# Summing the state outputs by accumulating transfers into two sums per chunk, with all steps written out

## The chip, the cores and the metric

One core of a Trainium2 chip runs the kernel. The metric is device time in microseconds (us), from the runs' own measurement; the profile is of one further execution of the same program. Engines are named as in the profile: PE (TensorE, matmuls), DVE (VectorE), ACT (ScalarE), POOL (GpSimd), SP (SyncE, which issues the plain transfers).

## What is computed

Four residual blocks over x of shape (4, 1024, 256), each followed by a layer norm: a gated linear recurrence, a ReLU feed-forward block, a selective state space block, and a second feed-forward block. The change lies in the third. Cut to what matters:

```python
dA  = exp(dt[..., None] * A)                    # (B, T, D, N), N = 16 states
dBx = dt[..., None] * B_ssm[:, :, None, :] * x_conv[..., None]
h_t = dA_t * h_(t-1) + dBx_t                    # a scan over time, for each channel and state
y_t = einsum('bdn,bn->bd', h_t, C_t)            # sum over the 16 states
y   = y * silu(z);  out = y @ out_proj_w.T
```

## The kernel before

The 4 sequences of 1024 tokens are cut into 8 chunks of 512 tokens (T). Channels lie on partitions: 256 channels are H = 2 halves of 128 partitions, so that a chunk's tile is 128 partitions x 1024 floats, 4 KB per partition and 512 KB in all. The program is software-pipelined over steps. In step i five stages of different chunks run side by side: *ahead* (chunk i+1: loads and first convolution), *gate* (chunk i: the recurrence of block one, out projection, first feed-forward up), *prep* (chunk i-1: feed-forward down, inputs of the state space block, the softplus for dt), *scan* (chunk i-2: the 16 states) and *tail* (chunk i-3: readout, out projection, second feed-forward, store). Each engine has its own instruction list; the function `step` of each engine writes out by hand in which order the pieces of these five stages follow one another, and semaphores tie the engines together. An engine works strictly in its order.

Four steps (3 to 6) are run by an engine loop of two turns (`Fori` in `steps`, two steps in a turn), the others are written out.

For one state n of a chunk in the scan stage:

- PE spreads the rows of B and C over 128 partitions into PSUM (L1287), ACT makes dA (L660).
- DVE `state_input` multiplies u by B into PSUM (L968, two instructions), `state_scan` runs the recurrence of both halves (L981), `state_output` multiplies the state by C into slot n % CRING of the ring hC (L994). The ring has CRING = 4 slots.
- POOL `sum_states` (L378) adds the slot to y, for n = 1 to 15: 15 additions of 128x1024 floats per chunk, each after the last. `state_output` of state n waits until the addition of state n-4 has read its slot:

```python
if n >= CRING:
    dve.wait_ge(S["y_sum"], ADDS * c + max(n - CRING, 1))
```

- DVE `readout` (L1000) multiplies the finished y by the gate, in the next step, after state 1 of the next chunk.

POOL also does, in the same hand-written order: the row scales of four layer norms (`row_scales`, L293 to L299, which wait for DVE's moments L843), the additions of two convolutions (`conv_add` L316, `mconv_add` L326), residuals and biases (L339, L342, L306), parts of log1p (`log1p_parts`, L350 to L360: maximum, minimum and two steps of a series) and the copies of the last state column (`save_carry` L386). In this order `sum_states(scan, 8)` stands behind the gate stage's `row_scales`, and `sum_states(scan, 9)` behind `log1p_parts`. DVE does, beside the states, the recurrence of block one (`log_A` L867, `recurrence` L903), moments of the layer norms (L836, L843), and a number of products of two SBUF tiles (L895, L936, L941, L951, L955, L1000).

Of the kernel before, what the change touches and what calls it, by code (L numbers as in the profile page):

```python
# [29 lines left out]
P = 128  # L30
D = 256
H = D // P
# [14 lines left out]
HRING = 2  # L47
CRING = 4
ARING = 4
BRING = 3  # L50
ADDS = NS - 1

# [12 lines left out]
LAGS = LAG_AHEAD, LAG_GATE, LAG_PREP, LAG_SCAN, LAG_TAIL = -1, 0, 1, 2, 3  # L65
LOOP_FIRST, LOOP_PAIRS = 3, 2


def build(nc, xT, x, par, ffb, rows, gateT, outT, inT, xpT, opT, w1a, w2a, w1b, w2b, out):
    ctx = ExitStack()  # L70
    with ctx:
# [57 lines left out]
        dt = sb("dt", [P, H, T])  # L129
        u = [sb(f"u{n}", [P, H, T]) for n in range(2)]  # L130

# [3 lines left out]
        carry = sb("carry", [P, NS, H])  # L135
        y = sb("y", [P, H, T])
        yg = sb("yg", [P, H, T])
# [25 lines left out]
        def input_banks(n):  # L163
# [11 lines left out]
            dt_ready u_ready  # L175
            B_mm C_mm dA_ready dBx_ready h_ready carry_saved hC_ready y_sum yg_ready eps_ready tau_set ln_tau_ready x3_seeded xtok_loaded passed
            op_mm x3T_mm x3T_ready x3b_ready up1_mm relu1 down1_mm stored""".split()
        S = {n: sem(n) for n in names}
        weight_loaded = {n: sem(f"{n}_loaded") for n in "gate xp out w1_0 w2_0 in op w1_1 w2_1".split()}
        xt_loaded = [sem(f"xt_loaded{n}") for n in range(2)]  # L180

        sum_ready, stats, meanvar, neg_ready, ve_ready, rstd_ready, shift_ready, norm_ready = (
# [5 lines left out]
        def steps(eng, step):  # L188


            def chunk(i):
                return (i // PER_SEQ, i % PER_SEQ) if 0 <= i < NCHUNK else None

            def straight(i):
                step(*(chunk(i - lag) for lag in LAGS))

            for i in range(LAG_AHEAD, LOOP_FIRST):
                straight(i)
            with eng.Fori(0, LOOP_PAIRS) as turn:
                for k in range(PER_SEQ):  # L200
                    def at(lag):
                        i = LOOP_FIRST + k - lag
                        return (turn + i // PER_SEQ, i % PER_SEQ)
                    step(*(at(lag) for lag in LAGS))
            for i in range(LOOP_FIRST + PER_SEQ * LOOP_PAIRS, NCHUNK + LAG_TAIL):
                straight(i)

        def apart(eng):


            eng.sem_inc(S["passed"], 1)

        def num(ch):
# [60 lines left out]
        def _(pool):  # L274
# [94 lines left out]
            def sum_states(ch, n):  # L369

                c = num(ch)
                if n == 1 and not first(ch):
                    pool.wait_ge(S["yg_ready"], c)
                pool.wait_ge(S["hC_ready"], UNITS * c + H * n + H)
                if n > 1:
                    pool.wait_ge(S["y_sum"], ADDS * c + n - 1)
                so_far = hC[:, 0, :, :] if n == 1 else y[:]
                nc.gpsimd.tensor_tensor(y[:], so_far, hC[:, n % CRING, :, :], ALU.add).then_inc(S["y_sum"], 1)  # L378

# [7 lines left out]

            def step(ahead, gate, prep, scan, tail):
                if scan is not None:
                    save_carry(scan, 0)  # L390
                    save_carry(scan, 1)
                    sum_states(scan, 1)
# [406 lines left out]
        def _(dve):  # L799
# [153 lines left out]
            def dt_x(ch):  # L953
                dve.wait_ge(S["dt_ready"], num(ch) + 1)
                V.scalar_tensor_tensor(out=u[ch[1]][:], in0=dt[:], scalar=0.5, in1=v[:], op0=ALU.mult,  # L955
                                       op1=ALU.mult).then_inc(S["u_ready"], 1)


            def state_input(ch, n):

                c = num(ch)
                if n == 0:
                    dve.wait_ge(S["u_ready"], c + 1)
                else:
                    dve.wait_ge(S["hC_ready"], UNITS * c + H * n)
                dve.wait_ge(S["B_mm"], NS * c + n + 1)
                for h in range(H):
                    V.tensor_tensor(input_banks(n)[h][:], u[ch[1]][:, h, :], B_bank(n)[:], ALU.mult).then_inc(S["dBx_ready"], 1)  # L968

# [14 lines left out]
            def state_output(ch, n):  # L984
                c = num(ch)
                dve.wait_ge(S["C_mm"], NS * c + n + 1)

                if n >= CRING:
                    dve.wait_ge(S["y_sum"], ADDS * c + max(n - CRING, 1))
                elif not first(ch):  # L990
                    dve.wait_ge(S["y_sum"], ADDS * c + n + 1 - CRING)
                for h in range(H):
                    dve.wait_ge(S["h_ready"], UNITS * c + H * n + h + 1)
                    V.tensor_tensor(hC[:, n % CRING, h, :], hs[:, n % HRING, h, :], C_bank(n)[:], ALU.mult).then_inc(S["hC_ready"], 1)  # L994

            def readout(ch, gate):
                if gate is not None:
                    dve.wait_ge(S["conv_sum"], PAD * (num(gate) + 1))
                dve.wait_ge(S["y_sum"], ADDS * (num(ch) + 1))
                V.scalar_tensor_tensor(out=yg[:], in0=y[:], scalar=0.5, in1=zz[ch[1]][:],  # L1000
                                       op0=ALU.mult, op1=ALU.mult).then_inc(S["yg_ready"], 1)
# [502 lines left out]
```

## Time and profile before

| | |
|---|---|
| time, median of 3 runs | 1121.71 us (1120.54 to 1122.82) |
| span of the profiled execution, first to last instruction | 1118.2 us |
| what lies around the span, against the median | 3.5 us |
| DVE busy | 911.4 us, 82% of the span |
| PE busy (matmul) | 831.4 us, 74% |
| POOL busy | 688.4 us, 62% |
| ACT busy | 634.9 us, 57% |
| bytes moved by DMA | 19.42 MB, 17 GB/s over the span |

The profile of before does not state the profiled execution's own total time apart from its span; the span and the median of the runs are 3.5 us apart. Busy shares are of the whole span. The scans of the eight chunks run from about 170 to 1058 us; before them the pipeline fills, after them the last chunk's tail stage stands alone.

### The profile page before, as it was taken

The numbers are of one execution on the slowest core, as the hardware profiler recorded it, in microseconds if no ns is written. First come the engines' busy times: TensorE is split into PE (matmuls) and PEld (weight loads), VectorE is DVE, ScalarE is ACT, GpSimd is POOL, SyncE is SP. The second block draws the span as 40 slices with busy tenths as digits, with TensorE's granted clock in tenths as the row PEclk, the third lists the DMA queues.
The fourth block names the chain that finished last, engine by engine and source line by source line (L and its number), as shares of the span: only waits on it lengthen the run. The fifth ranks groups of instructions, "written<-read, shape, count | busy, mean of one in ns | idle before, by whom it ended". The sixth has DMA issues, their size and how long they took to land. (4 is left out here: it accounts for less than half of the span.)

```text
span 1118.2 us, 9795 instructions
## 1 busy us (share of the span) xinstructions
PE 831.4 (74%) x2536; PEld 501.1 (45%) x2536; DVE 911.4 (82%) x1250; ACT 634.9 (57%) x1016; POOL 688.4 (62%) x460
## 2 busy tenths in 40 slices
PE   2368469647877997798869986988788888269376
PEld 1126226223634664465436543656354645035144
DVE  0303227999999999999999999999999999999911
ACT  3533564747376756686668657766746376334221
POOL 2131373669755995689567967796749575845410
PEclk9779769767988998899889989999988889559678
DMA  8000000000000010001000000001000000000000
GB/s 300 0 19 19 0 20 19 1 19 0 1 1 0 1 57 1 1 1 58 1 0 0 23 34 0 0 0 38 1 1 1 19 1 1 19 1 0 19 1 19
DMA packets 9219, 19.42 MB, mean 17 GB/s; under 512 B 1360, under 2 KB 3920, under 8 KB 9168
## 3 DMA queue, kind: packets, MB, share of 16 engines
q1 hardware_dynamic: 9168, 18.88, 5.0%
q14 instruction: 36, 0.29, 0.1%
q8 instruction: 15, 0.25, 0.1%
HBM read 14.68 MB, written 4.19 MB: 17 GB/s over the span
## 5 line engine op out<-in xcount | busy, mean ns | idle before, releaser
L378 POOL TENSOR_TENSOR y<-y,hC 128x1024 f32<-128x1024 f32 x112 | 295.3, 2637 | 56.5 <-DVE hC L994 53.5
L1287 PE MATMUL pBC<-stack,sel 97*128 97x512 f32 x256 | 156.5, 626 | 119.5 <-DVE hs L981 116.2
L660 ACT ACTIVATE dA<-dt,A_neg 128x512 f32<-128x512 f32 x256 | 174.1, 718 | 121.3 <-DVE hs L981 110.6
L1174 PE MATMUL pC<-w,hT 128*128 128x256 f32 x1024 | 233.2, 382 | 5.9 <-ACT hT L584 5.8
L1174 PEld LDWEIGHTS pC<-w,hT 128*128 128x128 f32 x1024 | 194.6, 191 | 42.2 <-ACT hT L584 10.6
L968 DVE TENSOR_TENSOR pBC<-u,pBC 128x512 f32<-128x512 f32 x256 | 164.6, 688 | 19.9 <-PE pBC L1287 17.9
L994 DVE TENSOR_TENSOR hC<-hs,pBC 128x512 f32<-128x512 f32 x256 | 161.1, 670 | 0.1
L981 DVE TENSOR_TENSOR_SCAN hs<-dA,carry,pBC 128x512 f32<-128x512 f32 x128 | 156.4, 1264 | 0.0
L981 DVE TENSOR_TENSOR_SCAN hs<-dA,pBC 128x512 f32<-128x512 f32 x128 | 148.5, 1201 | 2.0 <-POOL carry L386 1.2
L584 ACT ACTIVATE hT<-pA,ffb_sb 128x512 f32<-128x512 f32 x128 | 86.9, 686 | 97.2 <-PE pA L1167 97.0
L1287 PEld LDWEIGHTS pBC<-stack,sel 97*128 97x128 f32 x256 | 53.0, 207 | 193.9 <-DVE hs L981 165.6
L1167 PE MATMUL pA<-x1T,w 128*128 128x512 f32 x256 | 127.1, 646 | 1.7 <-ACT x1T L576 1.4
L1167 PE MATMUL pA<-tg,w 128*128 128x512 f32 x256 | 120.9, 609 | 0.7 <-ACT tg L576 0.7
L1174 PE MATMUL pC<-out_w,st 128*128 128x256 f32 x128 | 46.9, 546 | 56.8 <-DVE st L903 56.8
L293 POOL TENSOR_TENSOR ve<-mv,eps_rows 128x4 f32<-128x4 f32 x32 | 8.4, 263 | 120.0 <-DVE mv L843 120.0
L1167 PEld LDWEIGHTS pA<-x1T,w 128*128 128x128 f32 x256 | 53.4, 210 | 63.8 <-issue 60.1
L326 POOL TENSOR_TENSOR yg<-yg,v 128x1024 f32<-128x1024 f32 x24 | 59.9, 2496 | 33.4 <-ACT v L611 33.4
L316 POOL TENSOR_TENSOR conv<-conv,yg 128x1024 f32<-128x1024 f32 x24 | 56.6, 2356 | 37.2 <-ACT yg L505 37.2
L562 ACT ACTIVATE x<-x,shift,rstd 128x256 f32<-128x256 f32 x96 | 49.8, 589 | 51.4 <-POOL shift L299 51.4
L1167 PE MATMUL pA<-conv,gate_w 128*128 128x512 f32 x128 | 60.0, 616 | 21.5 <-POOL conv L316 21.5
L1167 PEld LDWEIGHTS pA<-tg,w 128*128 128x128 f32 x256 | 49.9, 196 | 53.3 <-issue 50.0
L1174 PEld LDWEIGHTS pC<-out_w,st 128*128 128x128 f32 x128 | 36.0, 289 | 70.8 <-issue 40.1
(118 smaller groups left out, 1256.8 us busy)
## 6 DMA issues: line engine op xcount, KB each, us to landing
xt<-xT SPq DMA_DIRECT2D x8, 515.0 KB, 5.1
xtok<-x SPq DMA_DIRECT2D x8, 512.0 KB, 4.5
out<-x3b SPq DMA_DIRECT2D x8, 512.0 KB, 2.9
w<-w1a SPq DMA_DIRECT2D x1, 1024.0 KB, 9.0
w<-w2a SPq DMA_DIRECT2D x1, 1024.0 KB, 11.3
w<-w1b SPq DMA_DIRECT2D x1, 1024.0 KB, 9.1
w<-w2b SPq DMA_DIRECT2D x1, 1024.0 KB, 10.9
gate_w<-gateT SPq DMA_DIRECT2D x1, 512.0 KB, 6.9
```

Of the source, the lines that this page charges most:

```text
L316: nc.gpsimd.tensor_tensor(conv[:], conv[:], tap[:], ALU.add).then_inc(S["conv_sum"], 1)
L326: nc.gpsimd.tensor_tensor(cv[:], cv[:], v[:], ALU.add).then_inc(S["mconv_sum"], 1)
L378: nc.gpsimd.tensor_tensor(y[:], so_far, hC[:, n % CRING, :, :], ALU.add).then_inc(S["y_sum"], 1)
L562: nc.scalar.activation(rows[:, b, :], rows[:, b, :], ACT.Identity, bias=shift[n][:, b:b + 1], scale=rstd[n][:, b:b + 1]).then_inc(norm_rea ...
L584: nc.scalar.activation(hT[:, f, :], pA[f % 2][:], ACT.Relu, bias=ffb_sb[:, layer, f:f + 1]).then_inc(done, 1)
L660: nc.scalar.activation(dA[:, k % ARING, :], dt[:, h, :], ACT.Exp, scale=A_neg[:, h, n:n + 1]).then_inc(S["dA_ready"], 1)
L968: V.tensor_tensor(input_banks(n)[h][:], u[ch[1]][:, h, :], B_bank(n)[:], ALU.mult).then_inc(S["dBx_ready"], 1)
L981: V.tensor_tensor_scan(hs[:, n % HRING, h, :], dA[:, k % ARING, :], input_banks(n)[h][:], 0.0 if p == 0 else carry[:, n, h:h + 1], ALU.mul ...
L994: V.tensor_tensor(hC[:, n % CRING, h, :], hs[:, n % HRING, h, :], C_bank(n)[:], ALU.mult).then_inc(S["hC_ready"], 1)
L1167: mm = nc.tensor.matmul(dst, w[:, k, lo:lo + dst.shape[0]], src(k), start=k == 0, stop=k == H - 1)
L1174: mm = nc.tensor.matmul(dst[:, b * D:b * D + D], src(k, t0), w[:, k, :], start=k == 0, stop=k == nk - 1)
L1287: return nc.tensor.matmul(dst[:], sel[0:NXK, row:row + 1].to_broadcast([NXK, P]), stack[ch[1]][0:NXK, :], start=True, stop=True)
```

## The change

The sum over the states is taken off POOL's arithmetic. States 0 and 1 are no longer written to the ring: `state_output` puts them directly into two sum buffers (`y_buf(c, 0)` and `y_buf(c, 1)`, out of three buffers y0 to y2 that rotate over the chunks). For n = 2 to 15 POOL issues a transfer from the ring slot to the sum buffer n % 2 with `accum_op=ALU.add`, 14 per chunk, 7 on each sum. Each transfer waits for the one before it on the same sum, since it reads and writes the same bytes. `sum_pair`, at the head of POOL's next step, waits for both sums and adds them with one 128x1024 addition; `readout` reads that. The ring hC has 3 slots instead of 4, and u one buffer instead of two. `state_output` of state n now waits for the landing of state n-3's transfer; state 1 waits for the addition of the chunk before. The order of everything else on POOL and DVE is as it was. The engine loop is gone: all steps are written out on every engine.

```diff
-CRING = 4
+CRING = 3
 ARING = 4
 BRING = 3
-ADDS = NS - 1
+ADDS = NS // 2 - 1
...
-        u = [sb(f"u{n}", [P, H, T]) for n in range(2)]
+        u = sb("u", [P, H, T])
...
-        y = sb("y", [P, H, T])
+        y = [sb(f"y{n}", [P, H, T]) for n in range(3)]
...
-            def straight(i):
+            for i in range(LAG_AHEAD, NCHUNK + LAG_TAIL):
                 step(*(chunk(i - lag) for lag in LAGS))
 
-            for i in range(LAG_AHEAD, LOOP_FIRST):
-                straight(i)
-            with eng.Fori(0, LOOP_PAIRS) as turn:
-                for k in range(PER_SEQ):
-                    def at(lag):
-                        i = LOOP_FIRST + k - lag
-                        return (turn + i // PER_SEQ, i % PER_SEQ)
-                    step(*(at(lag) for lag in LAGS))
-            for i in range(LOOP_FIRST + PER_SEQ * LOOP_PAIRS, NCHUNK + LAG_TAIL):
-                straight(i)
...
+        def y_buf(c, k):
+            return y[(2 * c + k) % 3]
+
+        def slot_user(n):
+            return max(m for m in range(2, NS) if m % CRING == n % CRING)
...
             def sum_states(ch, n):
 
-                c = num(ch)
-                if n == 1 and not first(ch):
-                    pool.wait_ge(S["yg_ready"], c)
+                if n < 2:
+                    return
+                c = num(ch)
                 pool.wait_ge(S["hC_ready"], UNITS * c + H * n + H)
-                if n > 1:
-                    pool.wait_ge(S["y_sum"], ADDS * c + n - 1)
-                so_far = hC[:, 0, :, :] if n == 1 else y[:]
-                nc.gpsimd.tensor_tensor(y[:], so_far, hC[:, n % CRING, :, :], ALU.add).then_inc(S["y_sum"], 1)
+                if n >= 4:
+                    pool.wait_ge(y_added[n % 2], 16 * (ADDS * c + n // 2 - 1))
+                pool.dma_start(y_buf(c, n % 2)[:], hC[:, n % CRING, :, :], accum_op=ALU.add).then_inc(y_added[n % 2], 16)
+
+            def sum_pair(ch):
+                c = num(ch)
+                for k in range(2):
+                    pool.wait_ge(y_added[k], 16 * ADDS * (c + 1))
+                nc.gpsimd.tensor_tensor(y_buf(c, 1)[:], y_buf(c, 1)[:], y_buf(c, 0)[:], ALU.add).then_inc(S["y_total"], 1)
...
             def step(ahead, gate, prep, scan, tail):
+                if tail is not None:
+                    sum_pair(tail)
                 if scan is not None:
                     save_carry(scan, 0)
...
             def dt_x(ch):
                 dve.wait_ge(S["dt_ready"], num(ch) + 1)
-                V.scalar_tensor_tensor(out=u[ch[1]][:], in0=dt[:], scalar=0.5, in1=v[:], op0=ALU.mult,
+                if not first(ch):
+                    dve.wait_ge(S["dBx_ready"], UNITS * num(ch))
+                V.scalar_tensor_tensor(out=u[:], in0=dt[:], scalar=0.5, in1=v[:], op0=ALU.mult,
...
@@ -985,19 +989,27 @@
                 c = num(ch)
                 dve.wait_ge(S["C_mm"], NS * c + n + 1)
 
-                if n >= CRING:
-                    dve.wait_ge(S["y_sum"], ADDS * c + max(n - CRING, 1))
+                if n == 0:
+                    if c >= 2:
+                        dve.wait_ge(S["yg_ready"], c - 1)
+                elif n == 1:
+                    if c >= 1:
+                        dve.wait_ge(S["y_total"], c)
+                elif n - CRING >= 2:
+                    dve.wait_ge(y_added[(n - CRING) % 2], 16 * (ADDS * c + (n - CRING) // 2))
                 elif not first(ch):
-                    dve.wait_ge(S["y_sum"], ADDS * c + n + 1 - CRING)
+                    before = slot_user(n)
+                    dve.wait_ge(y_added[before % 2], 16 * (ADDS * (c - 1) + before // 2))
+                dst = y_buf(c, n)[:] if n < 2 else hC[:, n % CRING, :, :]
                 for h in range(H):
                     dve.wait_ge(S["h_ready"], UNITS * c + H * n + h + 1)
-                    V.tensor_tensor(hC[:, n % CRING, h, :], hs[:, n % HRING, h, :], C_bank(n)[:], ALU.mult).then_inc(S["hC_ready"], 1)
+                    V.tensor_tensor(dst[:, h, :], hs[:, n % HRING, h, :], C_bank(n)[:], ALU.mult).then_inc(S["hC_ready"], 1)
...
             def readout(ch, gate):
                 if gate is not None:
                     dve.wait_ge(S["conv_sum"], PAD * (num(gate) + 1))
-                dve.wait_ge(S["y_sum"], ADDS * (num(ch) + 1))
-                V.scalar_tensor_tensor(out=yg[:], in0=y[:], scalar=0.5, in1=zz[ch[1]][:],
+                dve.wait_ge(S["y_total"], num(ch) + 1)
+                V.scalar_tensor_tensor(out=yg[:], in0=y_buf(num(ch), 1)[:], scalar=0.5, in1=zz[ch[1]][:],
                                        op0=ALU.mult, op1=ALU.mult).then_inc(S["yg_ready"], 1)
```

POOL's list around `log1p_parts`, in the scan of chunk 0 (before). The names are of tiles: tg, decay and inj are those of log1p, hC is the ring, y the sum, conv the first convolution.

```order
L378 TENSOR_TENSOR y<-y,hC 128x1024 [waits y_sum,hC_ready]
L350 TENSOR_SCALAR decay<-tg 128x1024 [waits e_ready]
L354 TENSOR_SCALAR tg<-tg 128x1024 [waits em_ready]
L358 TENSOR_SCALAR inj<-tg 128x1024 [waits es_ready]
L360 TENSOR_TENSOR inj<-inj,tg 128x1024 [waits p1_ready]
L386 COPY carry<-hs 128x2 [waits h_ready]
L378 TENSOR_TENSOR y<-y,hC 128x1024 [waits y_sum,hC_ready]
L386 COPY carry<-hs 128x2 [waits h_ready]
L378 TENSOR_TENSOR y<-y,hC 128x1024 [waits y_sum,hC_ready] x2
L316 TENSOR_TENSOR conv<-conv,yg 128x1024 [waits tap_ready,conv_sum]
L378 TENSOR_TENSOR y<-y,hC 128x1024 [waits y_sum,hC_ready]
```

And with the change, the same place:

```order
L372 DMA y<-hC 128x1024 [waits y_added0,hC_ready]
L345 TENSOR_SCALAR decay<-tg 128x1024 [waits e_ready]
L349 TENSOR_SCALAR tg<-tg 128x1024 [waits em_ready]
L353 TENSOR_SCALAR inj<-tg 128x1024 [waits es_ready]
L355 TENSOR_TENSOR inj<-inj,tg 128x1024 [waits p1_ready]
L386 COPY carry<-hs 128x2 [waits h_ready]
L372 DMA y<-hC 128x1024 [waits y_added1,hC_ready]
L386 COPY carry<-hs 128x2 [waits h_ready]
L372 DMA y<-hC 128x1024 [waits y_added0,hC_ready]
L372 DMA y<-hC 128x1024 [waits y_added1,hC_ready]
L311 TENSOR_TENSOR conv<-conv,yg 128x1024 [waits tap_ready,conv_sum]
```

Every addition y<-y,hC has become a transfer y<-hC at its old place; the one of state 8 still stands behind the row scales, the one of state 9 behind the four log1p instructions, and each waits for the transfer two states back (y_added0 or y_added1).

DVE's list of states 11 and 12 in the same chunk, before (scan instructions stand as SCALAR_TENSOR_TENSOR):

```order
L994 TENSOR_TENSOR hC<-hs,pBC 128x512 [waits h_ready,y_sum,C_mm]
L994 TENSOR_TENSOR hC<-hs,pBC 128x512 [waits h_ready]
L968 TENSOR_TENSOR pBC<-u,pBC 128x512 [waits B_mm,hC_ready]
L968 TENSOR_TENSOR pBC<-u,pBC 128x512
L981 SCALAR_TENSOR_TENSOR hs<-dA,pBC 128x512 [waits dA_ready,dBx_ready,carry_saved]
L981 SCALAR_TENSOR_TENSOR hs<-dA,pBC 128x512 [waits dA_ready,dBx_ready]
L994 TENSOR_TENSOR hC<-hs,pBC 128x512 [waits h_ready,y_sum,C_mm]
```

and with the change:

```order
L1006 TENSOR_TENSOR hC<-hs,pBC 128x512 [waits h_ready,y_added0,C_mm]
L1006 TENSOR_TENSOR hC<-hs,pBC 128x512 [waits h_ready]
L972 TENSOR_TENSOR pBC<-u,pBC 128x512 [waits B_mm,hC_ready]
L972 TENSOR_TENSOR pBC<-u,pBC 128x512
L985 SCALAR_TENSOR_TENSOR hs<-dA,pBC 128x512 [waits dA_ready,dBx_ready,carry_saved]
L985 SCALAR_TENSOR_TENSOR hs<-dA,pBC 128x512 [waits dA_ready,dBx_ready]
L1006 TENSOR_TENSOR hC<-hs,pBC 128x512 [waits h_ready,y_added1,C_mm]
```

Nothing moved here; the wait for POOL's sum has become a wait for a landing, and by the ring's size it is that of state n-3 (state 12 waits for state 9 on y_added1) where it was n-4.

## Rows read from the trace of the kernel before

**Rows 1.** Busy time by stretch, all engines; columns: stretch, length, busy us and count, clock.

```profile
500.00:600.00 100.00, 82.50 (x250) 48.39 (x249) 98.60 (x128) 64.83 (x107) 71.85 (x44) 0.91 0.05 17
...
800.00:900.00 100.00, 81.97 (x266) 53.27 (x265) 97.23 (x134) 52.89 (x88) 64.76 (x41) 0.88 0.02 6
```

**Rows 2.** DVE groups: out<-in, count, busy us, mean ns, idle before.

```profile
L903 DVE TENSOR_TENSOR_SCAN st<-decay,st,tg 128x512 f32<-128x512 f32 x16 | 36.9, 2343 | 0.1
...
L867 DVE TENSOR_TENSOR_SCAN st<-decay,st,clip 128x512 f32<-128x512 f32 x16 | 29.1, 1856 | 0.2
...
L936 DVE SCALAR_TENSOR_TENSOR inj<-inj,tg 128x1024 f32<-128x1024 f32 x8 | 20.0, 2504 | 14.5 <-POOL inj L360 14.5
...
L955 DVE SCALAR_TENSOR_TENSOR u<-dt,v 128x1024 f32<-128x1024 f32 x8 | 17.4, 2179 | 0.0
...
L951 DVE SCALAR_TENSOR_TENSOR dt<-tg,ln_tau,inj 128x1024 f32<-128x1024 f32 x8 | 16.4, 2049 | 2.9 <-POOL tg L367 2.9
L941 DVE SCALAR_TENSOR_TENSOR inj<-inj,tg 128x1024 f32<-128x1024 f32 x8 | 15.9, 1984 | 0.0
...
L1000 DVE SCALAR_TENSOR_TENSOR yg<-y,zz 128x1024 f32<-128x1024 f32 x8 | 9.7, 1217 | 2.5 <-POOL y L378 2.5
```

**Rows 3.** One line's instructions, DVE L867: shortest, median, longest ns.

```profile
L867 DVE TENSOR_TENSOR_SCAN st<-decay,st,clip x16: 1252/1258/3301, 31.0 to 783.9; 128x512 f32<-128x512 f32 x16
```

**Rows 4.** Timeline of POOL: start us, length us, line, tiles, count.

```profile
268.02 3.40 POOL L378 TENSOR_TENSOR y<-y,hC 128x1024 f32<-128x1024 f32 x1
...
605.60 0.20 POOL L293 TENSOR_TENSOR ve<-mv,eps_rows 128x4 f32<-128x4 f32 x1 [1.52 <-DVE mv L843]
...
607.30 2.35 POOL L378 TENSOR_TENSOR y<-y,hC 128x1024 f32<-128x1024 f32 x1
609.74 2.78 POOL L350 TENSOR_SCALAR decay<-tg 128x1024 f32<-128x1024 f32 x1
...
619.12 5.64 POOL L378 TENSOR_TENSOR y<-y,hC 128x1024 f32<-128x1024 f32 x2
...
640.00 5.79 POOL L378 TENSOR_TENSOR y<-y,hC 128x1024 f32<-128x1024 f32 x2
...
950.60 2.36 POOL L378 TENSOR_TENSOR y<-y,hC 128x1024 f32<-128x1024 f32 x1
```

**Rows 5.** Timeline of DVE, same stretches.

```profile
263.72 1.26 DVE L994 TENSOR_TENSOR hC<-hs,pBC 128x512 f32<-128x512 f32 x2
...
605.16 0.35 DVE L843 BATCH_NORM_AGGREGATE mv<-st 128x2 f32<-128x6 f32 x4
...
610.75 1.26 DVE L994 TENSOR_TENSOR hC<-hs,pBC 128x512 f32<-128x512 f32 x2
...
615.71 1.26 DVE L994 TENSOR_TENSOR hC<-hs,pBC 128x512 f32<-128x512 f32 x2
...
619.99 2.57 DVE L936 SCALAR_TENSOR_TENSOR inj<-inj,tg 128x1024 f32<-128x1024 f32 x1
...
637.58 1.27 DVE L994 TENSOR_TENSOR hC<-hs,pBC 128x512 f32<-128x512 f32 x2
...
650.74 1.25 DVE L994 TENSOR_TENSOR hC<-hs,pBC 128x512 f32<-128x512 f32 x2
...
948.22 1.26 DVE L994 TENSOR_TENSOR hC<-hs,pBC 128x512 f32<-128x512 f32 x2
```

**Rows 6.** POOL group of the state additions.

```profile
L378 POOL TENSOR_TENSOR y<-y,hC 128x1024 f32<-128x1024 f32 x112 | 295.3, 2637 | 56.5 <-DVE hC L994 53.5 <-issue 0.3
```

**Rows 7.** DMA queue and issues: packets, MB, share; KB each, us to landing.

```profile
q1 hardware_dynamic: 9168, 18.88, 5.0%
...
out<-x3b SPq DMA_DIRECT2D x8, 512.0 KB, 2.9
w<-w1a SPq DMA_DIRECT2D x1, 1024.0 KB, 9.0
```

**Rows 8.** Chain that ended last, its end: start us, length us, what.

```profile
1058.57 2.35 POOL y L378
```

More of the change, by code:

```diff
@@ L65 @@
 LAGS = LAG_AHEAD, LAG_GATE, LAG_PREP, LAG_SCAN, LAG_TAIL = -1, 0, 1, 2, 3
-LOOP_FIRST, LOOP_PAIRS = 3, 2
 def build(nc, xT, x, par, ffb, rows, gateT, outT, inT, xpT, opT, w1a, w2a, w1b, w2b, out):
@@ L175, in build @@
             dt_ready u_ready
-            B_mm C_mm dA_ready dBx_ready h_ready carry_saved hC_ready y_sum yg_ready eps_ready tau_set ln_tau_ready x3_seeded xtok_loaded passed
+            B_mm C_mm dA_ready dBx_ready h_ready carry_saved hC_ready y_total yg_ready eps_ready tau_set ln_tau_ready x3_seeded xtok_loaded passed
             op_mm x3T_mm x3T_ready x3b_ready up1_mm relu1 down1_mm stored""".split()
@@ L180, in build @@
         xt_loaded = [sem(f"xt_loaded{n}") for n in range(2)]
+        y_added = [sem(f"y_added{k}") for k in range(2)]
         sum_ready, stats, meanvar, neg_ready, ve_ready, rstd_ready, shift_ready, norm_ready = (
@@ L967, in state_input @@
                 for h in range(H):
-                    V.tensor_tensor(input_banks(n)[h][:], u[ch[1]][:, h, :], B_bank(n)[:], ALU.mult).then_inc(S["dBx_ready"], 1)
+                    V.tensor_tensor(input_banks(n)[h][:], u[:, h, :], B_bank(n)[:], ALU.mult).then_inc(S["dBx_ready"], 1)
             def state_scan(ch, n):
```

## The prediction

> **What bounds the kernel now.** I read the busy time by stretch first. While states are scanned, DVE works 98.60 of 100 us where the engine loop runs and 97.23 where the steps are written out; POOL 72 and 65, PE 82 [rows 1]. DVE therefore sets the pace, and only two things can move the time: how long DVE's own instructions take, and waits put in front of them. The written-out stretch has no fewer gaps than the looped one, so I cost the loop's removal at nothing; DVE's work covers branches on the others.
>
> Then DVE's groups. L1000 multiplies two 128x1024 SBUF tiles in 1217 ns; the same form takes 2504 (L936), 2179 (L955), 2049 (L951) and 1984 (L941). The scans over two SBUF operands take 2343 (L903) and 1856 (L867) on average [rows 2], and 1.252 at their shortest [rows 3]. What differs is the company: L936 at 619.99 took 2.57 us while POOL ran two additions from 619.12 to 624.76 [rows 4, 5]. DVE loses time when both engines read SBUF.
>
> Third, the two timelines of chunk 3, read side by side. DVE finishes the gate stage's moments (L843) at 605.5, POOL starts the row scales at 605.60, adds state 8 at 607.30 and runs log1p's parts from 609.74 to 619.12, where state 9 is added at last [rows 4]. DVE computes the output of state 11 at 610.75 and of state 12 at 615.71 [rows 5]. With four slots state 12 needs only the addition of state 8, long past. It writes **3.4 us before** state 9 is even begun.
>
> **The parts, and what each costs.**
>
> Removed: 15 additions of 2.64 us per chunk [rows 6], 316 us of POOL in all; one 128x1024 addition per chunk comes back, 21 us. POOL is not the bound, so this counts only through DVE. Excess over the undisturbed duration: L903 16 x (2343 - 1252) = 17.5 us, L867 16 x 604 = 9.7, L936 8 x 1287 = 10.3, L955 7.7, L951 6.7, L941 6.1: 58 us. POOL's other tile operations (log1p, convolutions, biases) cause part of it and stay. The additions are 46% of POOL's busy time (316 of 688), which gives 27; all of it would be 58. I take 36, above the plain share because L936 stood wholly beside additions. The Trainium skill ("SBUF — State Buffer", "Who interferes with whom") says that of two such instructions the later one to issue blocks fully until the first is done. The rows above do not bear that out: 2.57 us beside 5.6 us of additions is an excess of 1.35, not a whole addition, so the measurement decides; by the rule the relief would be nearer the 58.
>
> Added, issue: g, what POOL spends on one transfer. No row shows a transfer issued by POOL. Between its smallest instructions (0.2 us, [rows 4]) and an addition (2.6) I take 1.0, nearer the small ones since no tile passes through the engine.
>
> Added, landing: D, from issue until the sum may be used. Nearest rows: 512 KB stored from SBUF land after 2.9 us; 1024 KB of weights after 9.0 [rows 7]. An accumulation reads source and sum, 1 MB in all. Queue 1 moved 18.88 MB in 5.0% of 16 x 1118 us, which is 21 GB/s per engine or 340 GB/s, so a second 512 KB costs an estimated 1.5 us. 2.9 + 1.5 + 1.0 for the issue = 5.4; I take D = 5.5, ends 2.9 and 9.0. The Trainium skill ("DMA: Bandwidth & Descriptors", "Anatomy of one DMA — SWDGE (gpsimd) path") fits 2.0 us plus bytes at 436 GB/s, an estimate of 3.2 us for 512 KB. It speaks of copies, no run here shows it, and with it the sum below would fall by some 18 us.
>
> Wait at state 12, the term that decides. It now needs the landing of state 9's transfer, which keeps its place behind the row scales and log1p. POOL gets there earlier only by state 8's addition turned issue, 2.35 - g = 1.35. In chunk 3 the gap is 619.12 - 615.71 = 3.4, in chunk 0 268.02 - 263.72 = 4.3 [rows 4, 5]; chunks 0 to 5 lie at or between these, I take 3.7. DVE waits 3.7 - 1.35 + 5.5 = 7.85 us per chunk, six times: 47. Chunk 6 has no gate stage: 950.60 - 948.22 = 2.4, so 6.5. Chunk 7 has neither and waits for nothing, as its POOL is free. Together **54 us**. The wait at state 11 for state 8 (607.30 + 5.5 against 610.75, 2 us) lies inside it. Behind the waiting instruction on DVE stands everything, so nothing hides it; DVE has no gap to win it back, and PE (spreading B and C) and ACT (dA) wait with it.
>
> The pair. `sum_pair` waits for both sums, and state 1 of the next chunk waits for it. In the old trace POOL began 13 and 14 at 640.00, 2.4 us after DVE's state 15 at 637.58 [rows 4, 5], because it was behind. Freed of the additions it issues 13 before state 15 ends (638.9): 15 lands at 644.4, the pair is done at 646.8 and state 1 comes at 650.74. Cost nothing. If POOL stays as late as it was, 13, 15 and the pair end at 640 + 11 + 2.4 = 653.4, 2.7 us late, seven times 19: that is kept for the range.
>
> Ring and buffers: u with one buffer adds a wait for inputs DVE itself issued long before: nothing. States 0 and 1 written straight to the sums: the same product, nothing.
>
> The end. The last addition, 1058.57 for 2.35, lies on the chain that ended last [rows 8]. It becomes landing plus pair: + 5.5.
>
> **Sum.** + 54 + 5.5 - 36 = + 23 us. The profiled span 1118.2 becomes 1141.7; the runs' median stands 3.5 above that span, so 1121.7 becomes **1145**.
>
> **The rivals.**
>
> *Relief outweighs the wait (faster).* The place is the DVE instructions of [rows 2]. If the whole 58 us go, and the transfer lands like the store (D = 2.9, g = 0.2): 6 x (3.7 - 2.15 + 2.9) = 27, chunk 6 adds 3, the end 3, so 33 - 58 = - 25: 1097. Each us of D is worth 8 us (seven waits and the end). With 36 of relief it decides at D = 2.6, with 58 at D = 5.4. For it: those groups really do take up to twice their short time. Against: log1p, convolutions and biases still run beside them. 0.22.
>
> *Slow accumulation.* If reading two operands and adding makes D 9.0, like the 1 MB of weights: 6 x 11.35 + 10 + 9 = 87, with the late pair 19, less 36: + 70, 1192. Then POOL also stands in front of its own transfers (state 11 waits for 9), and row scales behind them come late. For it: nothing in this trace adds in a transfer. Against: the store's 2.9. 0.15.
>
> *Issue as dear as the addition (the change does not free POOL).* With g = 2.6 the 1.35 turns to - 0.25 and each wait grows by 1.6: + 11, 1156. Relief might still come, as no tile is read. 0.08, inside the range.
>
> The forecast itself has 0.55. Range 1105 to 1195: it takes in the slow case's 1192, and a good half of the way to 1097. About 0.2% (2 us) is what a measurement of this kernel can tell from no change. Faster 0.22 from the first rival; within 0.2%, 0.04, where relief and wait cancel; slower 0.74.
>
> **What the new profile would show.** Right: DVE's output product idle before it, released by a DMA, about 7 to 8 us once in each of chunks 0 to 6, at state 12; L936 and L867 nearer 1.2 us each; DVE's busy time down by about 36; POOL's down by some 300; the last readout 5 us later after the last state. Wrong: no DMA wait on DVE (then D is short, or POOL reaches state 9 earlier than its list allows), waits at nearly every state (then the landing is over 13 us, the time in which three states pass), L903 still at 2.3 (then the additions were not what slowed it), or a gap at each step's head where the loop was taken out.

## The result, and the profile after

| | before | after |
|---|---|---|
| time, median of 4 runs | 1121.55 us (1120.54 to 1122.82) | 1152.57 us (1151.71 to 1154.04) |
| span of the profiled execution | 1118.2 us | 1152.2 us |
| DVE busy | 911.4 us | 886.4 us |
| POOL busy | 688.4 us | 483.3 us |
| DVE idle, released by a transfer of the sum | none | 48.5 us, 13 times |

The changed kernel takes 1.0281 times as long (95% interval 1.0267 to 1.0296): 31 us more by the medians, 34.0 by the two spans. The forecast was 1145 in a range of 1105 to 1195. The sign and the mechanism held; three sizes did not: the landing, the relief, and the waits left out of the sum.

The page of the changed kernel: busy time by engine; the two costliest groups that the change touches (busy us, mean ns, idle before); the DMA queues (packets, MB, share of 16 engines); the issues (KB each, us to landing):

```profile
PE 826.9 (72%) x2536; PEld 497.0 (43%) x2536; DVE 886.4 (77%) x1250; ACT 636.1 (55%) x1016; POOL 483.3 (42%) x460
...
q0 software_dynamic: 16128, 58.73, 26.9%
q1 hardware_dynamic: 9168, 18.88, 5.1%
...
L1006 DVE TENSOR_TENSOR hC<-hs,pBC 128x512 f32<-128x512 f32 x224 | 141.1, 670 | 48.9 <-DMA y<-hC 48.5
...
L372 POOL DMA_DIRECT2D y<-hC x112 | 101.8, 927 | 133.2 <-DVE hC L1006 102.5
...
y<-hC POOLq DMA_DIRECT2D x112, 512.0 KB, 4.6
```

L1006 computes the state output. In the kernel before, nothing held it up (0.1 us idle in all); now it idles 48.5 us until a transfer has landed. POOL's additions [rows 6] have become 112 issues of 927 ns, and a transfer lands 4.6 us after its issue begins.

The stretches of [rows 1] again (length, busy us and count, clock, DMA share, GB/s):

```profile
500.00:600.00 100.00, 79.89 (x237) 46.28 (x236) 91.93 (x126) 60.31 (x96) 44.63 (x43) 0.91 0.39 79
800.00:900.00 100.00, 77.91 (x239) 45.46 (x238) 90.14 (x118) 62.51 (x102) 47.59 (x40) 0.91 0.39 77
```

DVE fell from 98.6 and 97.2 of 100 us to 91.9 and 90.1, while POOL is now idle more than half of the time. An engine that paced the kernel has been given gaps, by the one that was relieved.

DVE's waits (us in total, times, longest):

```profile
DVE hC L1006 <- DMA y<-hC: 48.5, 13, 5.7
DVE pBC L972 <- PE pBC L1299: 23.4, 19, 4.2
DVE yg L1012 <- POOL y L378: 7.4, 1, 7.4
DVE y L1006 <- POOL y L378: 2.3, 3, 1.1
```

In the kernel before, the wait ahead of the last readout was 2.5 us and the one for pBC (the rows of B and C that PE spreads) 17.9:

```profile
DVE pBC L968 <- PE pBC L1287: 17.9, 11, 4.2
```

So the span's + 34.0 is + 48.5 (landings) + 5.5 (pBC, from PE) + 4.9 (the last readout) + 2.3 (state 1 behind the pair) - 25.0 (DVE busy) and about - 2 of small differences.

Chunk 3 is the stretch of [rows 4, 5]. Two timelines of the changed kernel (start us, length us, line, tiles, count, idle before). POOL:

```profile
615.95 0.94 POOL L372 DMA_DIRECT2D y<-hC  x1 [0.30 <-issue]
616.97 2.78 POOL L345 TENSOR_SCALAR decay<-tg 128x1024 f32<-128x1024 f32 x1
...
624.03 2.35 POOL L355 TENSOR_TENSOR inj<-inj,tg 128x1024 f32<-128x1024 f32 x1
626.33 1.81 POOL L372 DMA_DIRECT2D y<-hC  x2
631.48 0.85 POOL L372 DMA_DIRECT2D y<-hC  x1 [3.34 <-DMA y<-hC]
632.04 2.66 POOL L311 TENSOR_TENSOR conv<-conv,yg 128x1024 f32<-128x1024 f32 x1
634.34 1.20 POOL L372 DMA_DIRECT2D y<-hC  x1
634.95 2.96 POOL L362 TENSOR_TENSOR tg<-tg,decay 128x1024 f32<-128x1024 f32 x1
```

DVE:

```profile
620.63 1.28 DVE L1006 TENSOR_TENSOR hC<-hs,pBC 128x512 f32<-128x512 f32 x2 [1.49 <-DMA y<-hC]
...
631.03 1.28 DVE L1006 TENSOR_TENSOR hC<-hs,pBC 128x512 f32<-128x512 f32 x2 [5.43 <-DMA y<-hC]
...
635.34 3.66 DVE L938 SCALAR_TENSOR_TENSOR inj<-inj,tg 128x1024 f32<-128x1024 f32 x1
```

State 11 (620.63) has waited 1.49 us for the transfer of state 8, issued at 615.95; state 12 (631.03) has waited 5.43 for that of state 9, issued at 626.33, behind all of log1p. Both go 4.7 us after the issue began. The two waits make 6.92 us, in the place where the prediction put 7.85. Chunks 0 to 5 all show this pair, 1.5 to 2.1 us and 5.4 to 5.7; chunk 6 shows the second alone, 5.3, and chunk 7 none: 38.6 us at state 12 and 9.9 at state 11.

Last, DVE's groups of [rows 2] as they stand now:

```profile
L905 DVE TENSOR_TENSOR_SCAN st<-decay,st,tg 128x512 f32<-128x512 f32 x16 | 27.9, 1781 | 0.1
...
L938 DVE SCALAR_TENSOR_TENSOR inj<-inj,tg 128x1024 f32<-128x1024 f32 x8 | 19.6, 2451 | 12.9 <-POOL inj L355 12.9
L869 DVE TENSOR_TENSOR_SCAN st<-decay,st,clip 128x512 f32<-128x512 f32 x16 | 19.5, 1262 | 0.2
L925 DVE SCALAR_TENSOR_TENSOR v<-v,yg 128x1024 f32<-128x1024 f32 x8 | 15.2, 1905 | 8.6 <-ACT v L622 8.6
L959 DVE SCALAR_TENSOR_TENSOR u<-dt,v 128x1024 f32<-128x1024 f32 x8 | 15.1, 1890 | 0.0
...
L943 DVE SCALAR_TENSOR_TENSOR inj<-inj,tg 128x1024 f32<-128x1024 f32 x8 | 14.0, 1755 | 0.0
L953 DVE SCALAR_TENSOR_TENSOR dt<-tg,ln_tau,inj 128x1024 f32<-128x1024 f32 x8 | 12.1, 1511 | 2.9 <-POOL tg L362 2.9
```

The clip scan (L867, now L869) is at its undisturbed 1.26 us; the gate scan (L903, now L905) fell from 2343 to 1781 ns; but L936, now L938, hardly moved (2504 to 2451), and L925 rose to 1905 ns. In the kernel before that product was L923:

```profile
L923 DVE SCALAR_TENSOR_TENSOR v<-v,yg 128x1024 f32<-128x1024 f32 x8 | 11.2, 1400 | 8.5 <-ACT v L620 8.5
```

### The profile page after: what moved, and what is told of

Read it like the earlier page. It is cut to its first block and busy times, and to the rows that moved or that the text cites. A ratio compares the mean times of both kernels' runs of the same rounds, so it can differ in the third digit from the quotient of the medians.

```text
span 1152.2 us, 8934 instructions
## 1 busy us (share of the span) xinstructions
PE 826.9 (72%) x2536; PEld 497.0 (43%) x2536; DVE 886.4 (77%) x1250; ACT 636.1 (55%) x1016; POOL 483.3 (42%) x460
## 3 DMA queue, kind: packets, MB, share of 16 engines
q0 software_dynamic: 16128, 58.73, 26.9%
## 5 line engine op out<-in xcount | busy, mean ns | idle before, releaser
L972 DVE TENSOR_TENSOR pBC<-u,pBC 128x512 f32<-128x512 f32 x256 | 164.6, 687 | 24.8 <-PE pBC L1299 23.4
L1006 DVE TENSOR_TENSOR hC<-hs,pBC 128x512 f32<-128x512 f32 x224 | 141.1, 670 | 48.9 <-DMA y<-hC 48.5
L372 POOL DMA_DIRECT2D y<-hC x112 | 101.8, 927 | 133.2 <-DVE hC L1006 102.5
L1179 PE MATMUL pA<-x1T,w 128*128 128x512 f32 x256 | 134.2, 678 | 1.4 <-ACT x1T L578 1.4
L1179 PEld LDWEIGHTS pA<-x1T,w 128*128 128x128 f32 x256 | 56.8, 223 | 67.9 <-issue 65.2
L311 POOL TENSOR_TENSOR conv<-conv,yg 128x1024 f32<-128x1024 f32 x24 | 60.1, 2504 | 52.1 <-ACT yg L507 51.8
L1186 PE MATMUL pC<-out_w,st 128*128 128x256 f32 x128 | 42.0, 501 | 48.3 <-DVE st L905 48.3
L386 POOL COPY carry<-hs 128x2 f32<-128x2 f32 x64 | 22.6, 354 | 96.0 <-DVE hs L985 96.0
```

Of the source, the lines that this page charges most:

```text
L311: nc.gpsimd.tensor_tensor(conv[:], conv[:], tap[:], ALU.add).then_inc(S["conv_sum"], 1)
L372: pool.dma_start(y_buf(c, n % 2)[:], hC[:, n % CRING, :, :], accum_op=ALU.add).then_inc(y_added[n % 2], 16)
L972: V.tensor_tensor(input_banks(n)[h][:], u[:, h, :], B_bank(n)[:], ALU.mult).then_inc(S["dBx_ready"], 1)
L1006: V.tensor_tensor(dst[:, h, :], hs[:, n % HRING, h, :], C_bank(n)[:], ALU.mult).then_inc(S["hC_ready"], 1)
L1179: mm = nc.tensor.matmul(dst, w[:, k, lo:lo + dst.shape[0]], src(k), start=k == 0, stop=k == H - 1)
L1186: mm = nc.tensor.matmul(dst[:, b * D:b * D + D], src(k, t0), w[:, k, :], start=k == 0, stop=k == nk - 1)
```

## The experiments

My theory: the loss is the *place* of state 9's transfer in POOL's list, with the landing behind it, on a ring one slot shorter; the relief of DVE is real but smaller than forecast. The rivals: the accumulation itself is slow whatever its place; or the loss comes from the written-out steps or from work on POOL that the transfers delay. Each ratio below is to runs of the kernel before that were measured beside it (medians 1119.8 to 1120.8 us).

### The loop alone (b_straight)

```diff
-            for i in range(LAG_AHEAD, LOOP_FIRST):
-                straight(i)
-            with eng.Fori(0, LOOP_PAIRS) as turn:
...
+            for i in range(LAG_AHEAD, NCHUNK + LAG_TAIL):
                 step(*(chunk(i - lag) for lag in LAGS))
```

> The kernel before with all steps written out and nothing else changed. Theory (the loop costs nothing where DVE is busy): within 0.2% of 1120, at most 1 us faster. Rival (writing the steps out costs instruction fetch): slower by over 2 us.

Measured: 1120.74 us (11 runs) against 1120.76 (15 runs), ratio 1.000 (0.9991 to 1.0009). Writing the steps out costs nothing and gives nothing.

### The relief alone (b_thin)

The kernel before, written out; from state 2 on, POOL's addition takes two columns per half, so that the order and the semaphores stay and the tile traffic goes. The sum over the states is therefore left out.

```diff
-                nc.gpsimd.tensor_tensor(y[:], so_far, hC[:, n % CRING, :, :], ALU.add).then_inc(S["y_sum"], 1)
+                nc.gpsimd.tensor_tensor(y[:] if n == 1 else y[:, :, 0:2], hC[:, 0, :, :] if n == 1 else y[:, :, 0:2], hC[:, 1, :, :] if n == 1 else hC[:, n % CRING, :, 0:2], ALU.add).then_inc(S["y_sum"], 1)
```

> The kernel before, steps written out, with 14 of the 15 additions per chunk cut to two columns per half (most of the sum over the states is left out). It measures the relief alone, without any transfer: theory, 25 us (what DVE's busy time fell by) to 38 us (what overlaps with the additions came to in the trace of before), so 1084 to 1097. If the relief were all of the 58 us of the prediction's list, 1063. If the additions do not slow DVE, 1121.

Measured: 1077.56 us (1076.10 to 1078.41), ratio 0.962 (0.9604 to 0.9636), 43 us less and below the range that I gave. DVE's busy time is 873.4 us, 38.0 less than before (36.8 less than in b_straight); the last readout waits 0.3 us in place of 2.5. POOL keeps an instruction for each addition (536 ns on average). The busy times:

```profile
PE 810.1 (75%) x2536; PEld 488.8 (45%) x2536; DVE 873.4 (81%) x1250; ACT 635.6 (59%) x1016; POOL 439.3 (41%) x460
```

This is about the ceiling of the whole idea: with the additions gone and nothing put in their place, the relief is 38 us of DVE and a few us of waits. The changed kernel got 25 of those 38.

### The later wait alone (b_wait3)

The kernel before, written out; the ring keeps its four slots, but output n waits for the addition of state n - 3, as with three slots.

```diff
-                    dve.wait_ge(S["y_sum"], ADDS * c + max(n - CRING, 1))
+                    dve.wait_ge(S["y_sum"], ADDS * c + max(n - 3, 1))
```

> The kernel before, steps written out, four slots and POOL's additions kept, but the output product of state n waits for the addition of state n-3 instead of n-4, as if the ring had three slots. Theory: the wait is made by order and ring, not by transfers: state 12 waits 3.7 + 2.35 = 6 us in six chunks and 4.8 in the seventh, less some contention that the wait avoids: 1150 to 1163. Rival (only the transfer makes the wait): 1121.

Measured: 1157.24 us (1156.55 to 1158.05), ratio 1.0327 (1.031 to 1.0344), inside the expected range. DVE's waits:

```profile
DVE hC L983 <- POOL y L367: 41.7, 7, 6.7
```

Seven waits, and no transfer into the sum in this run. The later wait alone, with the addition of state 9 behind log1p, costs 37 us; the whole change cost 31, with 25 us of relief in it. So the loss does not need a transfer: an answer by POOL at that place is too late for a ring of three, whoever gives it. With transfers the landing makes up more of it than the lateness does: in chunk 3 DVE would, without the two waits, have been ready for state 12 2.2 us before state 9's issue at 626.33, and the landing adds 4.7 to that: 6.9, the sum of the two waits.

### Moving two issues (a_order9, a_order)

The changed kernel with the issue of state 9 moved ahead of log1p:

```diff
                     sum_states(scan, 8)
+                    sum_states(scan, 9)
                 if prep is not None:
...
                     save_carry(scan, 11)
-                    sum_states(scan, 9)
                     save_carry(scan, 12)
```

> The changed kernel with one POOL instruction moved: the transfer of state 9 is issued right after that of state 8, before the log1p parts instead of behind them. Theory (late issue against a ring of three): state 12 no longer waits, state 11 still waits about 1.5 us in six chunks; the DMA wait of DVE falls from 48.5 to about 10 us and the time from 1152.6 to about 1114. Rival (the transfers themselves are slow or in each other's way): the wait only moves to another state, the time stays above 1145. Rival (the loop written out costs the time): no change.

Measured: 1107.93 us (1107.43 to 1111.38), ratio 0.9898 (0.9877 to 0.9919). This is 6 us less than expected. DVE's wait for landings:

```profile
DVE hC L1006 <- DMA y<-hC: 10.7, 7, 2.2
```

State 12's wait is gone, and state 11's is left, as expected. The median landing is still 4.6 us; issued in time, it is hidden. One moved line gives 45 us: 37.8 by this wait and 4.7 by the one for pBC, which fell from 23.4 to 18.7.

Then both issues ahead of the row scales:

```diff
-                if gate is not None:
-                    row_scales(LN_GATE, gate)
                 if scan is not None:
                     sum_states(scan, 8)
+                    sum_states(scan, 9)
+                if gate is not None:
+                    row_scales(LN_GATE, gate)
...
-                    sum_states(scan, 9)
```

> The changed kernel with the transfers of states 8 and 9 both issued before the gate stage's row scales and the log1p parts. Theory: no DMA wait of DVE is left, time about 1104 to 1108, so faster than the kernel before, since only the relief of DVE (25 us) and the longer end (5 us) remain. Cost to watch: the row scales come up to 2 us later and with them the normalisation of x1. Rival (slow transfers): above 1145.

Measured: 1101.34 us (1100.00 to 1102.05), ratio 0.9832 (0.9816 to 0.9849). DVE's groups and its first waits:

```profile
L938 DVE SCALAR_TENSOR_TENSOR inj<-inj,tg 128x1024 f32<-128x1024 f32 x8 | 19.4, 2421 | 12.2 <-POOL inj L355 12.2
...
L1006 DVE TENSOR_TENSOR hC<-hs,pBC 128x512 f32<-128x512 f32 x224 | 141.2, 673 | 3.3 <-DMA y<-hC 3.3
```

The time is 3 us below the expected range, although the waits for landings did not vanish: they are down to 3.3 us. The one for pBC is 14.6. What still stands between this and b_thin, 23.9 us of span: 11.6 us of DVE's busy time (885.0 against 873.4), 7.0 at the last readout, 3.3 of landings, 1.4 behind the pair. This is the fastest version that I ran with the whole sum in it, 19 us below the kernel before, with the accumulating transfers as they are.

### The landing (a_copy, a_half)

The changed kernel with plain transfers, so that the sum holds one state only and the additions are left out:

```diff
-                pool.dma_start(y_buf(c, n % 2)[:], hC[:, n % CRING, :, :], accum_op=ALU.add).then_inc(y_added[n % 2], 16)
+                pool.dma_start(y_buf(c, n % 2)[:], hC[:, n % CRING, :, :]).then_inc(y_added[n % 2], 16)
```

> The changed kernel with plain transfers in place of accumulating ones (the sums then hold only the last state's product; the adding is left out). It measures the second read. Step of the prediction: 1.5 us for it, so landing from 4.6 to about 3.1 us, and at 7 to 8 us of time per us of landing a time of about 1141. Rival (adding costs nothing beside the fixed part): landing and time unchanged, 1152.

And with accumulating transfers of the first half only (the second half's sum is left out):

```diff
+                pool.dma_start(y_buf(c, n % 2)[:, 0, :], hC[:, n % CRING, 0, :], accum_op=ALU.add).then_inc(y_added[n % 2], 16)
```

> The changed kernel with the accumulating transfer of one channel half only, 256 KB instead of 512 KB (the other half keeps the product of state 0 or 1: that half of the sum is left out). Theory (landing is a fixed part plus data): landing 4.6 falls by half of the data's time, 1.0 to 1.5 us, to 3.1 to 3.6, and the time by 7 to 12 us to about 1143. Rival (all fixed): 1152.

Measured: plain 1131.20 us (1129.74 to 1133.09), ratio 1.0092 (1.0075 to 1.0109), 10 us less than expected; half 1136.94 us (1135.06 to 1137.88), ratio 1.014 (1.0124 to 1.0156), 6 less. The page of the one with plain transfers:

```profile
q0 software_dynamic: 16128, 58.73, 12.7%
...
L1006 DVE TENSOR_TENSOR hC<-hs,pBC 128x512 f32<-128x512 f32 x224 | 141.1, 670 | 35.8 <-DMA y<-hC 35.8
...
L372 POOL DMA_DIRECT2D y<-hC x112 | 64.6, 577 | 132.5 <-DVE hC L1006 110.1
...
y<-hC POOLq DMA_DIRECT2D x112, 512.0 KB, 2.9
```

The page of the one with half the bytes:

```profile
q0 software_dynamic: 16128, 29.37, 15.0%
...
L372 POOL DMA_DIRECT2D y<-hC x112 | 101.5, 924 | 121.6 <-DVE hC L1006 101.7
...
y<-hC POOLq DMA_DIRECT2D x112, 256.0 KB, 3.3
```

For the same 58.73 MB the queue's engines are busy 26.9% of 1152.2 us when they accumulate and 12.7% of 1130.2 when they copy: 2.77 and 1.28 us per transfer of 512 KB, 1.5 us more. The landing grows by 1.7, from 2.9 to 4.6. The issue grows too, from 577 to 924 or 927 ns, and does so for 256 KB as for 512, so it goes with the kind of transfer, not with the bytes. The number of packets is 16128 in all three, so its part in the issue is not shown.

What the landing is worth in time: a_copy lands 1.7 us earlier; DVE waits 12.7 us less for landings (48.5 to 35.8) and 1.8 less at the end (7.4 to 5.6). That is 14.5 us, 8.5 per us of landing, close to the "each us of D is worth 8". DVE's busy time is 9.0 less (877.4 against 886.4), which I had not counted: 4.0 of it in the product v (L925) and 3.0 in L938, which met POOL's tile operations less or later. The two together are 23.5; the spans differ by 22.0, since the wait for state 1 behind the pair (2.3) went too, and others grew, that for pBC by 2.1 and that for decay (L861) by 1.7. Even with a copy's landing the kernel is slower than before; only the moved issues change the sign.

### Moving more (a_order_v2, a_order_v3)

I then tried to recover DVE's products, by moving POOL's remaining tile operations to where DVE has none. First, state 10's issue ahead of log1p and the gate's bias addition inside log1p, with `conv_add` 2 behind state 12 (each moved line leaves its old place):

```diff
+                if scan is not None:
+                    sum_states(scan, 8)
+                    sum_states(scan, 9)
                 if gate is not None:
                     row_scales(LN_GATE, gate)
                 if scan is not None:
-                    sum_states(scan, 8)
+                    sum_states(scan, 10)
...
                     log1p_parts(prep, 1)
+                if gate is not None:
+                    add_bias(LN_GATE, 0, x1, x1b, S["x1b_ready"], gate)
...
                     sum_states(scan, 11)
+                    sum_states(scan, 12)
```

> The kernel with states 8 and 9 issued early (1101.3), with POOL's remaining tile additions moved out of the way of DVE's two-operand products: state 10 issued before log1p, the gate stage's bias addition placed inside log1p, the second convolution addition behind the transfer of state 12. Theory (what is left of the relief is POOL's own tile operations meeting DVE's products): the log1p products of DVE (L938, L943) fall to 1.2 us in most chunks, DVE busy down by 8 to 12 us, time 1089 to 1094. Rival (transfers slow DVE): no change of DVE's busy time. Danger: the series product waits for log1p's end, or a late convolution addition delays the next gate stage.

Measured: 1104.10 us (1100.74 to 1105.02), ratio 0.9854 (0.9839 to 0.9869), not the 1089 to 1094 expected, and no better than a_order. DVE's waits:

```profile
DVE inj L939 <- POOL inj L355: 30.2, 8, 13.9
```

Its busy time did fall, from 885.0 in a_order to 871.8, the first version to reach b_thin's. But log1p now ends later, and the product L939 waits for it in every chunk: 30.2 us, where a_order had 12.2. The 18 us of wait took the 13 us of products back.

So log1p went back in one piece, with the issues and then the three tile operations behind it:

```diff
+                if scan is not None:
+                    sum_states(scan, 8)
+                    sum_states(scan, 9)
                 if gate is not None:
                     row_scales(LN_GATE, gate)
                 if scan is not None:
-                    sum_states(scan, 8)
+                    sum_states(scan, 10)
...
-                    sum_states(scan, 9)
...
                     sum_states(scan, 11)
+                    sum_states(scan, 12)
+                if gate is not None:
+                    add_bias(LN_GATE, 0, x1, x1b, S["x1b_ready"], gate)
```

> As a_order_v2, but the log1p parts stay in one piece and the gate stage's bias addition follows the transfers of states 11 and 12. What v2 showed: DVE's busy time fell by 13 us, and its series product then waited 18 us longer for log1p's end. Theory: the fall of the busy time stays (873 to 876 us) and the wait for log1p is back at 12 us, so 1101.3 - 10 = about 1090. If the bias addition meets the series product again, 1096.

Measured: 1125.26 us (1121.64 to 1128.90), ratio 1.0049 (1.003 to 1.0068). This was a plain miss, by 35 us (29 from the 1096 of its second case). The timeline of POOL in chunk 3:

```profile
616.78 1.80 POOL L372 DMA_DIRECT2D y<-hC  x2
618.02 2.95 POOL L301 TENSOR_TENSOR x1b<-x,rows_sb 128x1024 f32<-128x1024 f32 x1
620.33 2.92 POOL L311 TENSOR_TENSOR conv<-conv,yg 128x1024 f32<-128x1024 f32 x1
622.63 2.91 POOL L362 TENSOR_TENSOR tg<-tg,decay 128x1024 f32<-128x1024 f32 x1
```

and of DVE:

```profile
618.57 8.07 DVE L938 SCALAR_TENSOR_TENSOR inj<-inj,tg 128x1024 f32<-128x1024 f32 x1
626.56 2.44 DVE L985 TENSOR_TENSOR_SCAN hs<-dA,carry,pBC 128x512 f32<-128x512 f32 x2
```

The product L938, 1.2 us by itself, took 8.07: it started at 618.57, while POOL's L301 ran, and ended at 626.64, 1.1 us after the end of the *third* of POOL's three operations (622.63 + 2.91 = 625.54). It happened in two chunks (8.40 us in the other). Compared with a_order: DVE's busy time + 4.0 us, the wait for pBC + 10.9, for log1p + 6.8, behind the pair + 6.0, for landings - 2.5; together 25, against 23.8 of span.

## Why the prediction was right, and where its sizes were wrong

**"Wait at state 12, the term that decides": right.** Forecast 54 us; the trace shows 48.5 in 13 waits, twice in each of chunks 0 to 5 (state 11 for state 8, then state 12 for state 9), once in chunk 6, none in chunk 7. b_wait3 shows that the place in the list and the shorter ring make such a wait without any transfer, and a_order9 that moving this one issue takes 45 us back.

**"I take D = 5.5": 0.8 us too long, by the way it was added up.** Measured from issue to DVE's go: 4.7 us. The second read costs 1.5 us of engine time and 1.7 of landing, as estimated (1.5). The mistake is "+ 1.0 for the issue": the 2.9 us of the store's row already run from the issue, so the issue was counted twice. With 4.7 in the same formula, seven places fall by 5.6 us together, and 54 becomes 48, beside the 48.5 measured; the end falls from 5.5 to 4.7, beside 4.9.

The Trainium skill ("DMA: Bandwidth & Descriptors", "Anatomy of one DMA — SWDGE (gpsimd) path") gives a fit by which 512 KB take an estimated 3.2 us. The plain transfers of a_copy, at 2.9, come within 0.3 us of it; for the accumulating ones, at 4.6, it is 1.4 us short. The prediction had kept that reserve ("It speaks of copies").

**"I take g = 1.0": right**, 0.93.

**"I take 36" for the relief: too much for this order of POOL's list.** Measured 25.0. For the removal of the additions alone b_thin gives 38.0, close to the 36, but that is luck: the share it was taken from is no measure of the relief, as the next paragraph shows. What failed is the unspoken step that the *remaining* POOL operations would stay where they were in relation to DVE's products. Three of the groups moved as a relief should (busy time, rows of before first): the clip scan 29.1 to 19.5, the gate scan 36.9 to 27.9, the product of dt 16.4 to 12.1. Three more (u, L941 and L859, now L959, L943 and L861) gave 5.9 between them. L936, now L938, went only from 20.0 to 19.6, since L311 or L362 ran beside it in five of the eight chunks (635.34 above), and v rose by 4.0 us: POOL's L334 met it in three chunks (at 720.68 it took 3.25 us) and in one before. With the additions gone as well, b_thin has v at 11.2 us and a_copy too, so this meeting does not follow from a freed POOL alone; it turns on a few us in the two lists. The line "L936 and L867 nearer 1.2 us each" was thus half right.

**"The rows above do not bear that out": wrong, and the rule was right.** I had compared 2.57 us with *two* additions (5.6 us) and saw only 1.35 of excess. The timelines say more, read by their ends. POOL in the kernel before:

```profile
575.13 3.35 POOL L378 TENSOR_TENSOR y<-y,hC 128x1024 f32<-128x1024 f32 x1
578.44 3.25 POOL L326 TENSOR_TENSOR yg<-yg,v 128x1024 f32<-128x1024 f32 x1
```

DVE in the kernel before:

```profile
576.79 5.99 DVE L903 TENSOR_TENSOR_SCAN st<-decay,st,tg 128x512 f32<-128x512 f32 x2
```

The two scans, each 1.25 us alone, end at 582.78, which is 1.1 us after the end of L326 (578.44 + 3.25 = 581.69). The first takes 2.78 of it and ends at 579.57, again 1.1 after the end of the addition it had met (578.48). L938 in the changed kernel, 635.34 + 3.66 = 639.00, ends 1.1 after L362 (637.91); the 8.07 us of a_order_v3 end 1.1 after the third operation. And POOL pays as well: an operation of 2.36 us lasts 3.25 to 3.35 when DVE got in ahead of it. So the two do not slow each other down; one waits for the other's end. In the changed kernel 26 DVE products or pairs of scans are over 0.2 us longer than alone, and 25 of them end 1.07 to 1.10 us after a tile operation of POOL. The 1.35 of L936 at 619.99 is what was left of the *one* addition that had begun at 619.12 and would end at about 621.5.

The Trainium skill says just this ("SBUF — State Buffer", "Who interferes with whom"): a DVE instruction with two SBUF inputs and a GpSimd one that reads SBUF exclude each other, and the later waits out the earlier. The trace agrees, 2.57 us being the remaining 1.5 and 1.1 of its own. By this rule the excess of a DVE product is bounded by the remainder of one POOL operation, when DVE gets in between two; it does not grow with the share of time POOL is busy, so "46% of POOL's busy time" was no measure of the relief.

**"Cost nothing" for the pair: nearly right**, 2.3 us in 3 waits. **"Cost nothing" for the loop: right**, by b_straight. **PE:** "PE and ACT wait with it" left out that pBC comes later for states behind the wait; DVE waits 5.5 us more for it, and 3.3 us less than in the kernel before where the landings' waits are nearly gone (14.6 in a_order against 17.9). **"POOL's down by some 300"** contradicted the sum's own g: the 112 issues take 101.8 us where the additions took 295.3, and POOL fell by 205 in all.

The errors did not all point one way: the wait and the end 6 us too dear, the relief 11 too large, pBC and the pair 8 left out. Together that is 11 us on the span (+ 23 against + 34.0; 2 us of small differences went the other way), and 8 by the medians, since the median of before lies 3.5 us above its profiled span, that of after 0.4.

**Still open.** I did not try a ring of four slots with the transfers, which by this account should take state 12's wait away without moving an issue. The change gave a ring slot and a buffer of u for two more sum buffers, 4 KB per partition each, so it would need 4 KB more. In a_order, 11.6 us of products remain above b_thin and 7.0 at the last readout; no order that I tried had both the issues and the products right. Splitting POOL's operations so that DVE gets in was not tried.

## What to carry to other kernels

When work is taken off an engine that is not the bound, ask first which of its answers the bounding engine waits for, and at which place of its list each is given: here one line moved in that list was worth 45 us, nearly twice the relief of 25. Price a DVE product beside POOL by the end of the POOL instruction that it meets, not by the average share, and look at what POOL will run in the freed time. A ring that loses a slot turns an answer that was "long past" into one that comes too late, so do the sum again for every place where the answering engine is behind.

## What the runs showed of the hardware that I had not expected

- **An accumulating transfer takes twice the engine time of a copy.** 512 KB from SBUF to SBUF: 2.77 us of all 16 engines against 1.28 for a copy, landing after 4.6 us against 2.9, and 0.93 us of POOL for the issue against 0.58. With 256 KB it lands after 3.3, and the issue stays at 0.92.
- **Behind accumulating issues POOL's tile operations overlap in the records, and can lock DVE out together.** In the changed kernel a two-tile operation (L301, L311, L362) that follows such an issue at once starts 0.3 us before the issue's record ends and lasts 2.66 us instead of 2.36; after a second issue it is 0.6 us and 2.96. The POOL rows of chunk 3 show both: 631.48 + 0.85 = 632.33 against L311 at 632.04, and 634.34 + 1.20 = 635.54 against L362 at 634.95. With plain transfers it does not happen: in a_copy L311 and L362, just as close behind their issues, last 2.36 us. In a_order_v3 two issues stand ahead of L301, L311 and L362, the 0.6 us carries through all three, and DVE, which otherwise gets in after one operation, got in after three. In a_order_v2 the same two issues stand ahead of L311 (2.95) and L362 (2.95), and DVE's product had already gone ahead. So the overlap comes with the accumulating kind of issue. That such an issue still runs on part of POOL while the next instruction starts would explain it, but no run here shows that.
- **The transfers did not slow DVE's products.** With POOL issuing and the queue's engines busy 39% of the stretch, the clip scan stayed at 1262 ns on average, against 1252 at its shortest in the kernel before [rows 3], and the lengthened products end by POOL's tile operations, as said above, not by its issues.
